# Reordering the first batch of a fused attention-residual and FFN kernel: one root ahead of its gathers, mixing between additions, a square sum ahead of the gates, squared keys at other places

## The chip, the cores and the metric

The kernel runs on one core of one Trainium2 chip. The metric is the device time of one execution in microseconds; lower is better. The kernel before took 779.55 us, the median of three runs (778.33 to 780.54).

## The reference, cut to what matters

The input `x` has 16 batches of 512 rows with 512 columns, `ctx` has 16 batches of 512 rows with 1024 columns. All arithmetic is fp32.

```
x  = x + xattn(layernorm(x), ctx, patch_lens)
x  = x + ffn(layernorm(x))

xattn(e, c, lens):  h  = rmsnorm(e) @ W_in.T + b_in
                    hp = rmsnorm(c)[:, :512]             # mean square over all 1024 columns
                    s  = linear recurrence over rows:  s[t] = a * s[t-1] + gain * hp[t]
                    out[row] = s[plug[row]] + h[row]     # plug from cumulated patch_lens: a gather of rows
ffn(y):             y_prev = y shifted by one row
                    xr = mu_r*y + (1-mu_r)*y_prev ;  xk = mu_k*y + (1-mu_k)*y_prev
                    r  = sigmoid(xr @ W_r.T) ;  k = square(relu(xk @ W_k.T))
                    out = r * (k @ W_v.T)
```

## The kernel before, in words

**Tiling.** A batch is handled as four tiles of 128 rows (T = 4), and its 512 columns as four chunks of 128 (C = 4). Every fp32 product is made of three TensorE matmuls on parts in the type fp32r: high by high, high by low, low by high (`product`, L492 to L496). ScalarE makes the high part with a copy (`copy`, L715); VectorE makes the low part as whole minus high (`low`, L908). One "group" below is such a triple with 512 output columns.

**Stages of batch b.** *Projection* (`project`, L507): x times W_in, 16 groups. *Scan* (`scan`, L516): one group on the first 128 rows of ctx gives the recurrence; VectorE copies it out with the bias (`scan_out`, L914), ScalarE's queue stores it to DRAM (`s_rows`, L757), and GpSimd's queue gathers rows of it and adds them to x in `ring` (`add_patches`, L437, four indirect DMAs, L433). *Addition* (`add_x`, L1028): VectorE adds projection times `rs_a`, the reciprocal root of the first norm, which GpSimd makes (`root_a`, L391). *Second norm*: `stats_b`, `root_b` (L401), `norm_b`; TensorE turns it (`turn`, L589), ScalarE copies it out. *Mixing* (`mixing`, L1014, with ScalarE's `mix_hi`, L767): eight steps, four for xr (0 to 3) and four for xk (4 to 7). Then the *gate product* (xr by W_r, 16 groups), the *key product* (xk by W_k, 16 groups, L558), ScalarE's sigmoid (`gates`, L788) and its relu, square, high part of the keys (`squares`, L798), VectorE's low part of them (`ka_low`, L1064), and the *value product* (L574, 16 groups), whose first two row tiles come ahead of the next scan.

**ctx side.** `squares_c` (ScalarE, L748) squares the 128 x 1024 tile of ctx with a sum; `stats_c` (VectorE, L951), `root_c` (GpSimd, L403) and `scan_input` (VectorE, L957) make the scan's input `u`; `u_high` and `u_low` split it.

**Order.** Each engine executes its own instruction list in the order written out in its `iteration(b)`, with semaphores between engines. Iteration b handles the FFN of batch b, the projection's end and second norm of batch b+1 (`nxt`), and scan and gathers of batch b+2 (`new`). Iterations -1 and 0 are written out with branches of their own (`is_first`); 1 to 12 run in a hardware loop; the last three are written out. The change touches iterations -1 and 0 alone. There, W_r, W_k and W_v are still being split: W_v is staged in the tile `gate`, so `gates(0)` waits until VectorE has made all of `wv_lo` (`weight_lo(WV)`; L795). `squares(b)` of step m = 2 and 3 waits for `ka_low` of step m - 2, whose scratch it writes (L806).

**SyncE's queue**, iteration 0 (L325 to L340): when all four gathers of batch 1 have landed it issues the loads of batch 2: `xt` (1 MB), `ring` (1 MB), `ctx_rows` (0.5 MB), in this order:

```
rows_added(sp, new.plus(-1)) ; ... ; load_xt(new) ; ... ; load_x(new) ; ... ; load_ctx(new)
```

`squares_c(2)` waits for that last load (`reached(act, ctx_loaded, b, 16, 16)`, L749), `stats_c(2)` waits for `squares_c(2)` (L953). The key product's step m waits for `add_x(1, m)` (L566, it writes the bank that `add_x` reads) and at m = 0 chunk by chunk for xk's low parts (L569). The value product at row tile 0 waits for `ka_low(0, m)` before each m (L583).

Of the kernel before, what the change touches and what calls it, by code (L numbers as in the profile page):

```python
# [84 lines left out]
def build(nc, x, x_turned, ctx, patch_lens, w_in, b_in, columns, g_init, w_r, w_k, w_v, out):  # L85

    B, S, D = x.shape
# [11 lines left out]
    with ExitStack() as stack:  # L99
# [133 lines left out]
        def is_first(b, n=0):  # L233
            return b.fixed and b.number() == n
# [117 lines left out]
        def _(pool):  # L352
# [50 lines left out]
            def root_c(b):  # L403
                reached(pool, v_c_done, b, 1, 1)
                reached(pool, u_ready, b.plus(-1), 1, 1)
                nc.gpsimd.tensor_tensor(rs_c[:, :], v_c[:, 1:2], half[:, 0:1], ALU.pow).then_inc(rs_c_done, 1)
# [30 lines left out]
            def add_patches(b):  # L437

                rows_added(pool, b.plus(-1))
                nc.gpsimd.tensor_copy(patch_now[:, :], patch_of[:, bass.ds(b.number(), 1), :].rearrange("p a t -> p (a t)")  # L440
                                      ).then_inc(patch_picked, 1)

                reached(pool, bn_a_done, b, T, T)
                reached(pool, s_stored, b, 16, 16)
                reached(pool, patch_picked, b.plus(-1), 1, 1)
                hold(pool, pool_passed)
                for t in range(T):
                    add_rows(b, t, patch_now[:, t:t + 1])

            def iteration(b):  # L450
                nxt, new = b.plus(1), b.plus(2)
                if nxt.exists(B):
                    root_b(nxt)
                if is_first(b):
                    root_c(new)
                    root_a(new)
                elif new.exists(B) and not is_first(new, 1):
                    root_a(new)
                    root_c(new)
                if new.exists(B):  # L460
                    far(new)
                    add_patches(new)
                if is_first(nxt):
                    root_a(new)

            make_decay(0, P, 0)
            make_blocks()
# [245 lines left out]
        def _(act):  # L713
# [81 lines left out]
                        act.wait_ge(w_lo_ready[WV], C)  # L795
                    nc.scalar.activation(gate[:, t, :], bank[4 + t][:, :], ACT.Sigmoid).then_inc(gate_ready, 1)  # L796

            def squares(b):  # L798

                for m in range(C):  # L800
                    reached(act, k_done, b, C, m + 1)
                    if m == 0:
                        reached(act, mix_lo_ready, b, 2 * C, 2 * C)
                    if m >= 2:

                        reached(act, ka_lo_ready, b, C, m - 1)  # L806
                    nc.scalar.activation(scratch[:, m % 2, :], bank[m][:, :], ACT.Relu).then_inc(relu_ready, 1)  # L807
                    reached(act, relu_ready, b, C, m + 1)
                    nc.scalar.activation(scratch[:, 2 + m % 2, :], scratch[:, m % 2, :], ACT.Square).then_inc(square_ready, 1)  # L809
                    reached(act, square_ready, b, C, m + 1)  # L810
                    copy(ka(b)[0][:, m, :], scratch[:, 2 + m % 2, :]).then_inc(ka_hi_ready, 1)
# [12 lines left out]
            def iteration(b):  # L824
                nxt, new = b.plus(1), b.plus(2)
                if b.exists(B):
                    if is_last(b):
                        mix_hi(b, C, 2 * C)
                        squares(b)
                        gates(b)  # L830
                    elif is_first(b):
                        mix_hi(b, 0, C)
                        weight_hi(WK)
                        mix_hi(b, C, 2 * C)
                        weight_hi(WV)
                        gates(b)
                        squares_c(new)
                    else:
                        mix_hi(b, 0, 2 * C)
                        gates(b)  # L840
                        if new.exists(B):
                            squares_c(new)
                if is_first(b):
                    squares(b)
                    u_high(new)
                if new.exists(B) and not is_first(new, 1):
                    x_hi(new, 0)
                    x_hi(new, 1)
                if b.exists(B) and not is_last(b) and not is_first(b):
                    squares(b)  # L850
                if is_last(nxt):
                    turned_out(nxt)
                    mix_hi(nxt, 0, C)
                if is_first(nxt):
                    x_hi(new, 1)
                    squares_c(new)
                    u_high(new)
                    store_scan(new)
                    turned_out(nxt)
                elif new.exists(B):  # L860
                    if not is_first(b):
                        u_high(new)
                    store_scan(new)
                if nxt.exists(B) and not is_last(nxt) and not is_first(nxt):
                    turned_out(nxt)
# [29 lines left out]
        def _(dve):  # L895
# [173 lines left out]
            def iteration(b):  # L1069
                nxt, new = b.plus(1), b.plus(2)  # L1070
                if is_first(nxt):
                    stats_c(new)
                    for t in range(T):
                        add_x(nxt, t)
                        statistics_b(nxt, t)
                    stats_b(nxt, T)
                    scan_input(new)
                    u_low(new)
                    norm_b(nxt)
                    scan_out(new)  # L1080
                    far(new)
                    dve.sem_inc(far_over, 1)
                    stats_a(new)
                    return
                if b.exists(B):
                    mixing(b, C if is_last(b) else 0, 2 * C if is_last(b) else C + 1)
                if is_first(b):
                    weight_lo(WK)
                if nxt.exists(B):
                    add_x(nxt, 0)  # L1090
                    add_x(nxt, 1)
                if b.exists(B) and not is_last(b):
                    mixing(b, C + 1, 2 * C - 1)
                if nxt.exists(B):
                    add_x(nxt, 2)
                if b.exists(B) and not is_last(b):
                    mixing(b, 2 * C - 1, 2 * C)
                if is_first(b):
                    weight_lo(WV)
                if nxt.exists(B):  # L1100
                    add_x(nxt, 3)
                    stats_b(nxt)
                if is_first(b):

                    ka_low(b, 0)
                    stats_c(new)
                    ka_low(b, 1)
                    scan_input(new)
                    ka_low(b, 2)
                    stats_a(new)  # L1110
                    ka_low(b, 3)
                    u_low(new)
                    norm_b(nxt)
                    gating(b, 0)
                    gating(b, 1)
                    x_lo(new, 0)
                    x_lo(new, 1)
                    scan_out(new)
                    far(new)
                    dve.sem_inc(far_over, 1)  # L1120
                    add_out(b, 0)
                    add_out(b, 1)
                    gating(b, 2)
                    gating(b, 3)
                    add_out(b, 2)
                    add_out(b, 3)
                    return
                if new.exists(B):
                    stats_a(new)
                    stats_c(new)  # L1130
                if nxt.exists(B):
                    norm_b(nxt)
                for m in range(C):
                    if b.exists(B):
                        ka_low(b, m)
                    if new.exists(B):
                        if m in (1, 2):
                            x_lo(new, m - 1)
                        if m == 2:
                            scan_input(new)  # L1140
                if is_last(nxt):
                    mixing(nxt, 0, C)
                if new.exists(B):
                    u_low(new)
                if b.exists(B):
                    gating(b, 0)
                    gating(b, 1)
                if new.exists(B):
                    scan_out(new)
                    far(new)  # L1150
                    dve.sem_inc(far_over, 1)
                if b.exists(B):
                    add_out(b, 0)
                    add_out(b, 1)
                    gating(b, 2)
                    gating(b, 3)
                    add_out(b, 2)
                    add_out(b, 3)
# [131 lines left out]
```

## Time and profile before

| what | us |
|---|---|
| median of three runs | 779.55 |
| the profiled execution, its own time | 780.35 |
| its span (first to last instruction) | 778.8 |
| VectorE busy in the span | 556.2 |
| ScalarE busy | 413.7 |
| GpSimd busy | 175.5 |
| mean granted TensorE clock | 0.992 |

All times in views are from the start of the span, in microseconds. "Busy" of TensorE is modelled: matmuls are pipelined, and each shows about 0.39 us though a new one starts every 0.23 us. A timeline row gives start, duration, engine, source line, operation, tiles, count, and in brackets how long the engine had been idle before it and what released it. Landing times of DMAs are counted from the start of their issue. The granted clock is 1.00 at TensorE's full 2.4 GHz.

### The profile page before, as it was taken

Reading aid. Unit: us, or ns where it says so; the run is one execution under the profiler, and the core shown is the slowest. Engines: PE = TensorE matmul, PEld = TensorE weight load, DVE = VectorE, ACT = ScalarE, POOL = GpSimd, SP = SyncE. Lnnn points to the kernel's source line nnn. Section 1 sums busy time; section 2 is a strip of 40 time slices with the busy share of each in tenths; the row PEclk is TensorE's granted clock in tenths of the full one; section 3 lists DMA queues with packets and bytes.
Section 4 is the critical chain, followed back from the end, with each engine's and each line's share of the span. In section 5 each row is a group of like instructions: output and inputs, shape, how many; then the busy total and the mean of one; then the engine's idle time right before and its main releaser. Section 6 shows DMA issues by size and latency. Waiting matters only on the chain.

```text
span 778.8 us, 10909 instructions
## 1 busy us (share of the span) xinstructions
PE 755.4 (97%) x3462; PEld 621.9 (80%) x3463; DVE 556.2 (71%) x1005; ACT 413.7 (53%) x682; POOL 175.5 (23%) x175
## 2 busy tenths in 40 slices
PE   7878899999999999999999999999999999999997
PEld 4656688888888888888888888888888888888876
DVE  6797886766858677686776769577676967667552
ACT  4346565554546655455664545556454655544760
POOL 6622131313102131220313122131311213130000
PEclk9999999999999999999999999999999999999999
DMA  8556170524417053350705326071531706140011
GB/s 311 147 192 178 41 215 3 153 105 109 149 42 216 0 128 128 88 169 37 213 7 122 135 69 187 14 194 50 121 135 47 209 0 185 72 108 15 1 54 55
DMA packets 42765, 85.73 MB, mean 110 GB/s; under 512 B 3536, under 2 KB 3536, under 8 KB 42704
## 3 DMA queue, kind: packets, MB, share of 16 engines
q1 hardware_dynamic: 30768, 63.74, 21.8%
q0 software_dynamic: 9216, 16.78, 13.6%
q10 hardware_dynamic: 2736, 4.73, 1.8%
q8 instruction: 14, 0.23, 0.1%
q14 instruction: 31, 0.25, 0.1%
HBM read 64.26 MB, written 21.76 MB: 110 GB/s over the span
## 4 chain that ended last, share of the span: by engine, by line
PE 88%; DVE 4%; DMA 2%; issue 2%; ACT 2%; POOL 1%; SPq 0%; DVEq 0%; ACTq 0%; POOLq 0%
PE bank L494 28%; PE bank L495 28%; PE bank L496 28%; PE bank L599 3%; DMA xt<-in_x_turned 1%; POOL ring L433 1%; DMA s_rows<-scanned 1%; DMA ctx_rows<-in_ctx 1%; DVE ring L1034 1%; DVE xk_lo L908 1%; DVE scratch L1004 0%; DVE gate L1062 0%; ACT scratch L809 0%; DVE bn_a L937 0%; ACT scratch L807 0%
## 5 line engine op out<-in xcount | busy, mean ns | idle before, releaser
L433 POOL DMA_INDIRECT ring<-s_rows,patch_now x60 | 101.7, 1695 | 262.7 <-DMA s_rows<-scanned 231.0
L908 DVE TENSOR_TENSOR xr_lo<-scratch,xr_hi 128x512 fp32r<-128x512 f32 x124 | 85.6, 690 | 70.3 <-ACT xr_hi L715 69.8
L1004 DVE SCALAR_TENSOR_TENSOR scratch<-turned,cols,scratch 128x512 f32<-128x512 f32 x128 | 94.5, 749 | 31.5 <-ACT scratch L764 24.9
L715 ACT ACTIVATE turned<-bank 128x512 f32<-128x512 f32 x64 | 33.2, 604 | 137.1 <-PE bank L599 133.5
L494 PE MATMUL bank<-wi_hi,xt_hi 128*128 128x512 f32 x256 | 102.1, 399 | 3.3 <-DVE xt_lo L908 2.7
L494 PE MATMUL bank<-xk_hi,wk_hi 128*128 128x512 f32 x256 | 100.1, 391 | 3.4 <-DVE xk_lo L908 3.4
L494 PE MATMUL bank<-wr_hi,xr_hi 128*128 128x512 f32 x256 | 99.7, 390 | 1.0 <-DVE xr_lo L908 1.0
L495 PE MATMUL bank<-wi_lo,xt_hi 128*128 128x512 f32 x256 | 100.4, 392 | 0.0
L496 PE MATMUL bank<-wi_hi,xt_lo 128*128 128x512 f32 x256 | 100.2, 391 | 0.0
L496 PE MATMUL bank<-xk_hi,wk_lo 128*128 128x512 f32 x256 | 99.6, 389 | 0.0
L495 PE MATMUL bank<-xk_lo,wk_hi 128*128 128x512 f32 x256 | 99.6, 389 | 0.0
L496 PE MATMUL bank<-wr_hi,xr_lo 128*128 128x512 f32 x256 | 99.6, 389 | 0.0
L495 PE MATMUL bank<-wr_lo,xr_hi 128*128 128x512 f32 x256 | 99.6, 389 | 0.0
L494 PE MATMUL bank<-wv_hi,xr_hi 128*128 128x512 f32 x240 | 94.5, 394 | 2.0 <-DVE xr_lo L908 2.0
L495 PE MATMUL bank<-wv_lo,xr_hi 128*128 128x512 f32 x240 | 94.1, 392 | 0.0
L496 PE MATMUL bank<-wv_hi,xr_lo 128*128 128x512 f32 x240 | 94.0, 392 | 0.0
L764 ACT ACTIVATE scratch<-turned,cols 128x512 f32<-128x512 f32 x128 | 89.4, 710 | 0.5
L1062 DVE TENSOR_TENSOR gate<-bank,gate 128x512 f32<-128x512 f32 x64 | 43.9, 691 | 62.3 <-PE bank L496 62.3
L715 ACT ACTIVATE xr_hi<-scratch 128x512 fp32r<-128x512 f32 x124 | 77.9, 628 | 17.6 <-DVE scratch L1004 15.2
L796 ACT ACTIVATE gate<-bank 128x512 f32<-128x512 f32 x64 | 37.7, 595 | 86.0 <-PE bank L496 86.0
L715 ACT ACTIVATE xk_hi<-scratch 128x512 fp32r<-128x512 f32 x64 | 40.4, 632 | 49.3 <-DVE scratch L1004 48.5
L401 POOL TENSOR_TENSOR rs_b<-v_b,half 128x4 f32<-128x4 f32 x16 | 17.0, 1064 | 218.0 <-DVE v_b L1049 218.0
(134 smaller groups left out, 1283.4 us busy)
## 6 DMA issues: line engine op xcount, KB each, us to landing
ring<-in_x SPq DMA_DIRECT2D x16, 1024.0 KB, 7.4
out<-gate SPq DMA_DIRECT2D x64, 256.0 KB, 2.1
xt<-in_x_turned SPq DMA_DIRECT2D x14, 1024.0 KB, 5.2
ctx_rows<-in_ctx SPq DMA_DIRECT2D x16, 512.0 KB, 8.0
s_rows<-scanned ACTq DMA_DIRECT2D x16, 256.0 KB, 2.4
gate<-in_L_xattn_W_in SPq DMA_DIRECT2D x4, 256.0 KB, 6.2
xt<-in_x_turned SPq DMA_DIRECT2D x2, 512.0 KB, 8.0
ring<-in_x_turned SPq DMA_DIRECT2D x1, 1024.0 KB, 12.9
```

Source lines behind the costliest of these rows:

```text
L401: nc.gpsimd.tensor_tensor(rs_b[:, :, 0], v_b[:, :, 0], half[:, :], ALU.pow).then_inc(rs_b_done, 1)
L433: pool.indirect_dma_start(ring[b.slot][:, t, :], None, s_rows[:, :], bass.IndirectOffsetOnAxis(ap=rows, axis=0), compute_op=ALU.add).then_ ...
L494: nc.tensor.matmul(where, lhs_hi, rhs_hi, start=start, stop=False)
L495: nc.tensor.matmul(where, lhs_hi, rhs_lo, start=False, stop=False)
L496: return nc.tensor.matmul(where, lhs_lo, rhs_hi, start=False, stop=stop)
L599: last = nc.tensor.transpose(first_bank(b, t)[:, tile(c)], normed[:, t, c * P:(c + 1) * P], ident[:, :])
L715: return nc.scalar.activation(to, of, ACT.Copy)
L764: nc.scalar.activation(scratch[:, i % 2, :], turned[:, c, 0:S], ACT.Copy, scale=cols[:, 3 + which, c:c + 1]).then_inc(carried, 1)
L796: nc.scalar.activation(gate[:, t, :], bank[4 + t][:, :], ACT.Sigmoid).then_inc(gate_ready, 1)
L908: return nc.vector.tensor_tensor(to, whole, high, ALU.subtract)
L1004: nc.vector.scalar_tensor_tensor(scratch[:, 2 + i % 2, :], turned[:, c, 1:S + 1], cols[:, 1 + which, c:c + 1], scratch[:, i % 2, :], ALU.m ...
L1062: nc.vector.tensor_tensor(gate[:, t, :], bank[4 + t][:, :], gate[:, t, :], ALU.mult).then_inc(gated, 1)
```

## The change

Five moves, all in iterations -1 and 0; nothing is added or removed, only the order within the engines' lists differs.

- GpSimd, iteration -1: `root_a(1)` stands ahead of `add_patches(1)`, that is ahead of the four gathers, and no longer behind them.
- GpSimd, iteration 0: `root_c(2)` stands ahead of `root_b(1)`.
- ScalarE, iteration 0: `squares_c(2)` stands ahead of `gates(0)` (both behind `weight_hi(WV)`); `u_high(2)` stands between `squares` steps 1 and 2 and no longer behind step 3.
- VectorE, iteration 0: `add_x(1,0)`, mixing steps 5 to 7 in one piece, `add_x(1,1)`, `weight_lo(WV)`, `add_x(1,2)`, `add_x(1,3)`.
- VectorE, after that: `stats_c(2)` ahead of `stats_b(1)`, then `scan_input(2)`, `ka_low 0`, `stats_a(2)`, `ka_low 1`, `u_low(2)`, `ka_low 2`, `ka_low 3`.

```diff
@@ gpsimd iteration @@
                 nxt, new = b.plus(1), b.plus(2)
+                if is_first(b):
+                    root_c(new)
                 if nxt.exists(B):
                     root_b(nxt)
                 if is_first(b):
-                    root_c(new)
                     root_a(new)
...
                     far(new)
+                    if is_first(nxt):
+                        root_a(new)
                     add_patches(new)
-                if is_first(nxt):
-                    root_a(new)
@@ scalar @@
-            def squares(b):
+            def squares(b, first=0, last=C):
-                for m in range(C):
+                for m in range(first, last):
...
                         weight_hi(WV)
+                        squares_c(new)
                         gates(b)
-                        squares_c(new)
...
                 if is_first(b):
-                    squares(b)
+                    squares(b, 0, 2)
                     u_high(new)
+                    squares(b, 2, C)
@@ vector iteration, is_first(b) @@
                     weight_lo(WK)
-                if nxt.exists(B):
                     add_x(nxt, 0)
+                    mixing(b, C + 1, 2 * C)
                     add_x(nxt, 1)
-                if b.exists(B) and not is_last(b):
-                    mixing(b, C + 1, 2 * C - 1)
-                if nxt.exists(B):
+                    weight_lo(WV)
                     add_x(nxt, 2)
-                if b.exists(B) and not is_last(b):
-                    mixing(b, 2 * C - 1, 2 * C)
-                if is_first(b):
-                    weight_lo(WV)
-                if nxt.exists(B):
                     add_x(nxt, 3)
+                    stats_c(new)
                     stats_b(nxt)
-                if is_first(b):
+                    scan_input(new)
                     ka_low(b, 0)
-                    stats_c(new)
+                    stats_a(new)
                     ka_low(b, 1)
-                    scan_input(new)
+                    u_low(new)
                     ka_low(b, 2)
-                    stats_a(new)
                     ka_low(b, 3)
-                    u_low(new)
                     norm_b(nxt)
```

The general branch of VectorE's iteration keeps its order; it is only written below the first batch's own list.

## Rows read from the trace of the kernel before

**Rows 1.** The page, part 1: busy time, share of span, instructions.
```profile
PE 755.4 (97%) x3462; PEld 621.9 (80%) x3463; DVE 556.2 (71%) x1005; ACT 413.7 (53%) x682; POOL 175.5 (23%) x175
```
**Rows 2.** Waits of PE from 97 to 779: total, times, longest.
```profile
PE bank L494 <- DVE xk_lo L908: 1.2, 1, 1.2
```
**Rows 3.** Timeline of PE: start, duration, what, idle before.
```profile
65.14 0.39 PE L496 MATMUL bank<-wr_hi,xr_lo 128*128 128x512 f32 x1
66.35 0.47 PE L494 MATMUL bank<-xk_hi,wk_hi 128*128 128x512 f32 x1 [0.82 <-DVE xk_lo L908]
...
70.37 0.48 PE L494 MATMUL bank<-xk_hi,wk_hi 128*128 128x512 f32 x1
...
79.08 0.39 PE L496 MATMUL bank<-xk_hi,wk_lo 128*128 128x512 f32 x1
79.86 0.47 PE L494 MATMUL bank<-wv_hi,xr_hi 128*128 128x512 f32 x1 [0.39 <-DVE xr_lo L908]
...
83.40 0.50 PE L494 MATMUL bank<-wv_hi,xr_hi 128*128 128x512 f32 x1 [0.85 <-DVE xr_lo L908]
...
89.23 0.39 PE L494 MATMUL bank<-u_hi,decay_hi 128*128 128x512 f32 x1
```
**Rows 4.** Stretches: length, busy of the engines, granted clock, DMA share, GB/s.
```profile
80.50:84.00 3.50, 1.87 (x8) 1.00 (x7) 2.71 (x5) 3.37 (x7) 0.00 (x0) 1.00 0.00 0
...
84.50:87.50 3.00, 3.00 (x8) 2.33 (x8) 2.81 (x10) 2.34 (x3) 0.95 (x1) 0.50 0.00 0
```
**Rows 5.** Timeline of DVE, batch 1's first statistics to batch 2's.
```profile
51.76 0.17 DVE L948 TENSOR_SCALAR v_a<-mv_a 128x4 f32<-128x4 f32 x1
...
58.35 2.49 DVE L908 TENSOR_TENSOR wk_lo<-ring,wk_hi 128x512 fp32r<-128x512 f32 x4
63.53 1.41 DVE L1034 SCALAR_TENSOR_TENSOR ring<-bank,rs_a,ring 128x512 f32<-128x512 f32 x2 [2.68 <-POOL rs_a L395]
...
73.28 2.46 DVE L1039 BATCH_NORM_STATS2 bn_b<-ring 128x6 f32<-128x512 f32 x4
...
79.03 0.69 DVE L908 TENSOR_TENSOR xr_lo<-scratch,xr_hi 128x512 fp32r<-128x512 f32 x1 [2.54 <-ACT xr_hi L715]
...
82.65 0.69 DVE L908 TENSOR_TENSOR xr_lo<-scratch,xr_hi 128x512 fp32r<-128x512 f32 x1 [0.46 <-ACT xr_hi L715]
83.26 2.47 DVE L937 BATCH_NORM_STATS2 bn_a<-ring 128x6 f32<-128x512 f32 x4
...
86.38 0.68 DVE L908 TENSOR_TENSOR xr_lo<-scratch,xr_hi 128x512 fp32r<-128x512 f32 x1
```
**Rows 6.** Timeline of POOL: first gather of batch 1, its root.
```profile
54.78 1.79 POOL L433 DMA_INDIRECT ring<-s_rows,patch_now  x1 [8.71 <-DMA s_rows<-scanned]
...
61.76 1.64 POOL L395 TENSOR_TENSOR rs_a<-v_a,half 128x4 f32<-128x4 f32 x1
```
**Rows 7.** DMA issues from 54 to 66: median us to landing.
```profile
ring<-s_rows,patch_now POOLq DMA_INDIRECT x4, 4.8
```
**Rows 8.** Timeline of SP: the loads of batch 2.
```profile
66.26 0.37 SPq L293 DMA_DIRECT2D xt<-in_x_turned  x1
...
67.23 0.50 SPq L296 DMA_DIRECT2D ctx_rows<-in_ctx  x1
```
**Rows 9.** DMA issues from 66 to 76: size, us to landing.
```profile
ctx_rows<-in_ctx SPq DMA_DIRECT2D x1, 512.0 KB, 8.3
```
**Rows 10.** The tile ctx_rows, 0 to 130: its loads' time to landing.
```profile
DMA to landing us min/median/max: 4.6/8.1/8.3
```
**Rows 11.** Timeline of ACT: table load, square sum of ctx, first relu, first high part.
```profile
72.78 1.28 ACT L796 ACT_TABLE_LOAD   x1 [1.13 <-DVE wv_lo L908]
...
76.00 1.08 ACT L751 ACTIVATE ctx_squared<-ctx_rows 128x1024 bf16<-128x1024 f32 x1
...
77.05 0.62 ACT L807 ACTIVATE scratch<-bank 128x512 f32<-128x512 f32 x1
...
78.36 0.63 ACT L715 ACTIVATE xr_hi<-scratch 128x512 fp32r<-128x512 f32 x1
```

More of the change, by code:

```diff
@@ L1127, in iteration @@
                     return
+                if nxt.exists(B):
+                    add_x(nxt, 0)
+                    add_x(nxt, 1)
+                if b.exists(B) and not is_last(b):
+                    mixing(b, C + 1, 2 * C - 1)
+                if nxt.exists(B):
+                    add_x(nxt, 2)
+                if b.exists(B) and not is_last(b):
+                    mixing(b, 2 * C - 1, 2 * C)
+                if nxt.exists(B):
+                    add_x(nxt, 3)
+                    stats_b(nxt)
                 if new.exists(B):
```

## The prediction

> **What bounds the kernel now.** I read the page first: TensorE is busy in 97% of the span [rows 1]. Then the waits of TensorE after the first batches: from 97 us to the end there is one, of 1.2 us [rows 2]. So from there on the product stream is unbroken, and whatever the change does to the time must be done before it: a shift of TensorE's work at about 89 us is carried to the end one for one. The other question is only where batch 0's stream has holes, and TensorE's timeline has them all [rows 3]. The gate product ends at 65.14 + 0.23 = 65.4. The key product starts at 66.35, and its fourth group only at 70.37; from there 38 pitches lead to its last matmul at 79.08, (79.08 - 70.37) / 38 = 0.229 us each, so a group costs 0.69. The value product starts at 79.86 and its third group at 83.40. From there to batch 2's scan at 89.23 stand six groups, 4.1 us at full pitch, and 5.8 were taken. The stretches say why: in 80.5 to 84.0 TensorE is busy for 1.87 of 3.5 us, then the granted clock is 0.50, the lower level of 1.2 GHz, in 84.5 to 87.5 [rows 4]. All holes between 65.4 and 83.4 together: 18.0 us less 18 groups of 0.69 (12.4), thus 5.6, and 1.7 for the clock.
>
> **The change, part by part.**
>
> *The root ahead of the gathers and mixing between additions.* VectorE ends wk_lo at 60.8 and then waits 2.68 us for rs_a, which GpSimd makes behind four gathers [rows 5, 6]. Its input v_a was ready at 51.76 + 0.17 = 51.9 and GpSimd idle [rows 5, 6], so with the root first, at 1.64 us, rs_a is there by about 53.6. The first gather starts at 54.78 and lands 4.8 later, at 59.6 [rows 6, 7]. So add_x(1,0) runs at 60.8, and mixing steps 5 to 7 follow with nothing but themselves: with add_x(1,0) eight instructions of 0.7 us (1.41 for two [rows 5]), to 66.4, with the first xk low at about 62.8, the second 64.2, the third 65.5, the last 66.4. The key product takes its chunks at 65.4, 66.1, 66.8 and 67.4: no hole. It ends at 65.4 + 16 x 0.69 = 76.4 and not at 79.3: 2.9 us sooner. Its later steps need add_x(1,1) at 68.1 (done 67.0), add_x(1,2) at 70.9 (wv_lo goes before it, four instructions like wk_lo's 2.49 [rows 5]: wv_lo done 69.4, the addition 70.1) and add_x(1,3) at 73.6 (done 70.8). The margin at step 2 is 0.8.
>
> The gathers wait for the root, and for the copy of patch_now behind it (4 columns, as the root has, so at most another 1.64): 52.0 to between 53.6 and 55.3, where the first gather started at 54.78 [rows 6]. They move by 0 to 0.5 us. I take nothing, as a plain copy of 4 columns should be well under the root, and keep 0.5 for the range.
>
> *The square sum ahead of the gates.* This is where I expect the loss. squares_c(2) needs the load of ctx_rows. SyncE issues it third of three, after the last gather of batch 1 has landed: xt at 66.26, ctx at 67.23, and it lands 8.3 us after that, at 75.5 [rows 8, 9]. In the kernel before ScalarE is in the gates till 76.00 and finds it there 0.5 us old [rows 11]. Nothing in the change issues it sooner, because the gathers, which the issue follows, start when the scan is stored. Now ScalarE gets to squares_c(2) at about 68, when the last xk high part (65.7) and four copies of wv_hi (0.63 at most each [rows 11]) are out, and stands there for over 7 us. Behind it in its list: the table load and four gates (72.78 to 76.00, 3.22 us, [rows 11]), which could have begun at 69.4 with wv_lo done, and then the squared keys. So:
>
> - squares_c(2) starts at 75.6; it takes 77.05 - 76.00 = 1.05: 76.6.
> - table load and gates 3.22: first relu at 79.9 (before 77.05).
> - relu to high part 78.36 + 0.63 - 77.05 = 1.94 [rows 11]: 81.8. VectorE makes the low part at 81.85, TensorE's first value group follows 0.83 later (79.86 - 79.03 [rows 3, 5]): 82.7 (before 79.86).
>
> *stats_c(2) ahead of stats_b(1).* It makes VectorE wait for the same load, till 76.7. Behind it stand stats_b(1) (four statistics, four small ones and one more, built like stats_a, so 3.12 as worked out below) and scan_input(2) (one instruction like an addition, 0.7): done at 80.5, before the high part of 81.8 is there, so this costs nothing as long as ScalarE is late as well. root_b(1) moves behind it to about 80; norm_b(1), its reader, comes at 89.
>
> *Squared keys' lows.* stats_a(2), 86.38 - 83.26 = 3.12 us [rows 5], now stands between ka_low 0 and ka_low 1, where TensorE waits for each. A low part takes 83.26 - 82.65 = 0.61. ka_low 1 starts at 81.85 + 0.61 + 3.12 = 85.6; u_low and ka_low 2 follow at 86.2 and 86.8. TensorE's third value group follows its low part by 83.40 - 82.65 = 0.75: 87.5, against 83.40. High part 2 is there: relu 1 at 81.7, u_high (a copy of 0.63, as in [rows 11]) from 83.6, relu 2 at 84.1, high part 86.0. Step 3 starts once ka_low 1 is out (86.2), its low part is done at 89.0, and TensorE asks for it at 87.5 + 4 x 0.69 = 90.3. u_low is no longer late for anything.
>
> *Sum.* The third value group comes 87.5 - 83.4 = 4.1 us later, although the key product ended 2.9 earlier: TensorE's holes grow from 5.6 to 9.7 us. For the way from there to the scan I keep the 5.8 us with the low clock in it, as TensorE again stands before it, longer than before. norm_b(1) and scan_out(2) come some 4 us later on VectorE, as TensorE itself does, so nothing new is late for TensorE. So +4.1: span 778.8 to 782.9, the profiled execution's 780.35 to 784.45. That execution lies 0.8 over the median; on the median the forecast is 779.55 + 4.1 = 783.65 us.
>
> *Bounds.* Clock: if no low stretch falls on the six groups, 1.7 us less; if all 18 matmuls are at half speed, 18 x 0.229 = 4.1 over full pitch, 2.4 more than now. Landing of ctx: each us moves the end by one; the loads of this tile took 4.6 to 8.3 [rows 10]. 4.6 would put the landing at 71.8, the end 3.7 sooner. I take 8.3, which is this very load, behind 2 MB in the same queue. Its end can't be much later. Table load: up to 1.28 less if it should run under the wait, which the program order speaks against.
>
> On this the trace shows one load of 1.28 us, after an idle of 1.13, with the gates right behind it [rows 11]. The Trainium skill (ScalarE: Activation LUTs, "What ACT_TABLE_LOAD costs") gives every switch a drain of about 1380 ns beside the 1283 ns of the load. The load agrees; a drain is not seen in the gates' row, but it could have lain in the idle before the load. In the changed kernel the load stands right behind squares_c(2), and such a drain would be in the open: by that page the sum would be 1.4 more, 785.0. I go by the row.
>
> **Rivals.**
>
> *A: the load of ctx is there in time, and the holes close.* It decides at the landing: the third value group comes 12.0 us after it (87.5 - 75.5), so any landing before 71.4 is a gain. With ctx there at 67.7 the gates would end at 69.4 + 3.2 = 72.6, the first high part at 74.5. VectorE would be done with add_x(1,3) at 70.8, stats_b and scan_input at 74.6, ka_low 0 at 75.2; the first value group follows the key product at 76.4; ka_low 1 after stats_a at 78.4, third group at 80.4 (83.4 before): 3.0 less, and 4.7 with the clock held: 774.9 to 776.6. For it: the key product does end 2.9 sooner. Against it: the landing is 4 us off [rows 8, 9], and even the shortest load of this tile misses the point by 0.4.
>
> *B: the wait is there, but most of it is given back.* The low stretch ends within the long hole (-1.7) and the load is a little early (up to -1): +1.4 to +2.3, 781 to 781.9, no measurable change. For it: the hole before the first value group is over 6 us, long enough to hold a stretch of the 3 us seen. Against it: TensorE does only two groups between 82.7 and 87.5, which is less than it did before the drop at 84.
>
> *C: the clock stays low until the scan.* Up to 2.4 more than now, and the gathers up to 0.5 later: +5.3 to +7.0, 784.8 to 786.5. For it: two holes in a row. Against: in the kernel before it was low for 3 us only, with TensorE fully busy in them [rows 4].
>
> **How the numbers follow.** Forecast 0.60, A 0.09, B 0.15, C 0.16. This kernel's measurement tells some 0.3%, 2.3 us, from no change: the bounds are 777.2 and 781.9. Faster 0.09 (A); within 0.13 (most of B); slower 0.78. The range for 8 in 10 leaves out A and the end of C: 780.7 to 786.0. The forecast's own range is 782.5 to 784.8.
>
> **What would show it.** rs_a before the first gather and no hole of TensorE between 65.4 and 76.4 would show the first step right. ScalarE idle for some 8 us before ctx_squared, released by the DMA, and the first relu at about 80 show the second; ctx_rows issued much before 67 or landed before 71.4 would make the forecast wrong. A hole of over 6 us before the first value group and one near 3 us before its second, with stats_a(2) in VectorE's row between, show the third. If the granted clock is 1.00 from 87.5 on, the end comes 1.7 us sooner than forecast.

## The result, and the profile after

The changed kernel takes 784.65 us (median of five runs, 783.69 to 786.57); the kernel before, run beside it, 779.53 (777.85 to 780.54). The ratio is 1.0066, interval 1.0052 to 1.0080: 5.1 us slower, by the interval 4.1 to 6.2. Forecast were 783.7 us and +4.1, with a range from 780.7 to 786.0. The profiled execution took 784.65 with a span of 783.1, against 780.35 and 778.8: +4.3. The median lies inside the range, and inside the forecast's own of 782.5 to 784.8.

TensorE's timeline in batch 0, to be laid beside [rows 3]; columns as there:

```profile
65.53 0.39 PE L495 MATMUL bank<-xk_hi,wk_hi 128*128 128x512 f32 x1
...
76.18 0.39 PE L497 MATMUL bank<-xk_hi,wk_lo 128*128 128x512 f32 x1
82.62 0.77 PE L495 MATMUL bank<-wv_hi,xr_hi 128*128 128x512 f32 x1 [6.05 <-DVE xr_lo L910]
...
86.24 0.80 PE L495 MATMUL bank<-wv_hi,xr_hi 128*128 128x512 f32 x1 [2.00 <-DVE xr_lo L910]
...
87.69 0.63 PE L495 MATMUL bank<-wv_hi,xr_hi 128*128 128x512 f32 x1
...
93.55 0.39 PE L495 MATMUL bank<-u_hi,decay_hi 128*128 128x512 f32 x1
```

The key product has no hole and ends at 76.4, 2.9 us sooner than before. Then TensorE stands for 6 us and once more for 2 (forecast: near 3; the first group ran at half speed and filled 0.7 of it); the third value group comes at 87.69 (before 83.40), the scan at 93.55 (before 89.23). ScalarE, beside [rows 11], shows for whom it stands:

```profile
75.41 1.06 ACT L752 ACTIVATE ctx_squared<-ctx_rows 128x1024 bf16<-128x1024 f32 x1 [7.57 <-DMA ctx_rows<-in_ctx]
76.37 0.19 ACT L752 ACTIVATION_READ_ACCUMULATOR ctx_squared<-ctx_rows 128x1 f32 x1
76.57 1.28 ACT L797 ACT_TABLE_LOAD   x1
77.87 2.06 ACT L797 ACTIVATE gate<-bank 128x512 f32<-128x512 f32 x4
79.79 0.63 ACT L808 ACTIVATE scratch<-bank 128x512 f32<-128x512 f32 x1
```

7.57 us idle, released by the load of ctx, with the table load, the gates and the squared keys in line behind it. The load itself is where it was, beside [rows 8, 9]:

```profile
66.29 0.37 SPq L293 DMA_DIRECT2D xt<-in_x_turned  x1
...
67.26 0.50 SPq L296 DMA_DIRECT2D ctx_rows<-in_ctx  x1
```
```profile
ctx_rows<-in_ctx SPq DMA_DIRECT2D x1, 512.0 KB, 8.1
```

VectorE, beside [rows 5], waits for the same load ahead of stats_b(1), and has stats_a(2) between the first two lows:

```profile
60.91 0.74 DVE L1036 SCALAR_TENSOR_TENSOR ring<-bank,rs_a,ring 128x512 f32<-128x512 f32 x1
...
76.59 0.15 DVE L957 TENSOR_SCALAR v_c<-v_c 128x1 f32<-128x1 f32 x1 [5.72 <-ACT ctx_squared L752]
76.66 2.46 DVE L1041 BATCH_NORM_STATS2 bn_b<-ring 128x6 f32<-128x512 f32 x4
...
81.78 0.69 DVE L910 TENSOR_TENSOR xr_lo<-scratch,xr_hi 128x512 fp32r<-128x512 f32 x1 [1.25 <-ACT xr_hi L716]
82.39 2.47 DVE L939 BATCH_NORM_STATS2 bn_a<-ring 128x6 f32<-128x512 f32 x4
...
85.50 0.68 DVE L910 TENSOR_TENSOR xr_lo<-scratch,xr_hi 128x512 fp32r<-128x512 f32 x1
```

The granted clock, beside [rows 4] (length; busy us of PE, PEld, DVE, ACT, POOL; clock; DMA share; GB/s), is at the lower level of 1.2 GHz for longer than before, but most of it lies on idle time:

```profile
76.50:80.50 4.00, 0.07 (x1) 0.00 (x0) 3.72 (x11) 3.94 (x8) 1.13 (x2) 1.00 0.00 0
80.50:84.00 3.50, 1.38 (x3) 0.84 (x3) 2.25 (x5) 3.40 (x7) 0.91 (x1) 0.59 0.02 5
84.00:88.00 4.00, 2.00 (x5) 1.39 (x5) 3.20 (x10) 3.47 (x7) 1.76 (x2) 0.50 0.01 2
88.00:92.00 4.00, 4.00 (x12) 3.10 (x12) 2.52 (x5) 2.09 (x3) 0.00 (x0) 0.58 0.00 0
```

The same stretch of the kernel before that holds its low clock:

```profile
84.00:88.00 4.00, 4.00 (x12) 3.14 (x11) 3.81 (x11) 2.84 (x4) 1.45 (x2) 0.57 0.00 0
```

With only two levels, a mean of 0.57 over 4.0 us is 3.4 us at the lower one. After the change the rows add up to 2.9 + 4.0 + 3.4 = 10.2 us (about 81.2 to 91.4), of which 3.7 us lie behind the start of the third group.

### The profile page after: what moved, and what is told of

Read it like the earlier page. It is cut to its first block, busy times and chain, and to the rows that moved or that the text cites. A ratio compares the mean times of both kernels' runs of the same rounds, so it can differ in the third digit from the quotient of the medians.

```text
span 783.1 us, 10909 instructions
## 1 busy us (share of the span) xinstructions
PE 756.2 (97%) x3462; PEld 623.7 (80%) x3463; DVE 556.3 (71%) x1005; ACT 413.8 (53%) x682; POOL 176.0 (22%) x175
## 4 chain that ended last, share of the span: by engine, by line
PE 87%; DMA 3%; issue 3%; DVE 3%; ACT 1%; POOL 1%; SPq 0%; DVEq 0%; POOLq 0%; ACTq 0%
PE bank L495 28%; PE bank L496 28%; PE bank L497 28%; PE bank L600 3%; DMA ctx_rows<-in_ctx 2%; DMA xt<-in_x_turned 1%; DMA ring<-s_rows,patch_now 1%; DVE bn_a L939 1%; POOL ring L433 1%; DVE gate L1064 0%; DVE xk_lo L910 0%; DVE scratch L1006 0%; DVE gate L935 0%; ACT turned L716 0%; SPq L299 0%
## 5 line engine op out<-in xcount | busy, mean ns | idle before, releaser
L1006 DVE SCALAR_TENSOR_TENSOR scratch<-turned,cols,scratch 128x512 f32<-128x512 f32 x128 | 94.5, 749 | 34.6 <-ACT scratch L765 17.7
L716 ACT ACTIVATE turned<-bank 128x512 f32<-128x512 f32 x64 | 33.4, 605 | 138.4 <-PE bank L600 138.3
L1064 DVE TENSOR_TENSOR gate<-bank,gate 128x512 f32<-128x512 f32 x64 | 43.9, 690 | 65.2 <-PE bank L497 65.2
```

The lines of the kernel that those rows point to most:

```text
L716: return nc.scalar.activation(to, of, ACT.Copy)
L1006: nc.vector.scalar_tensor_tensor(scratch[:, 2 + i % 2, :], turned[:, c, 1:S + 1], cols[:, 1 + which, c:c + 1], scratch[:, i % 2, :], ALU.m ...
L1064: nc.vector.tensor_tensor(gate[:, t, :], bank[4 + t][:, :], gate[:, t, :], ALU.mult).then_inc(gated, 1)
```

## The experiments

**How the traces are compared.** The start of the program varies from execution to execution: VectorE copies batch 1's scan out (L919 or L921, later lines where a kernel has more) between 46.5 and 49.2 us, in kernels that don't differ ahead of it. From the scan of batch 2 to the end of the span, on the other hand, it is 778.8 - 89.23 = 689.6 us before, 783.1 - 93.55 = 689.6 after, and 689.5 to 689.9 in all ten experiments. So what a kernel did is read from the stretch between the two, counted from the copy's start. "Chain" is from squares_c(2)'s start to the third value group. Two limits: each column of times comes from one execution of each kernel, and the medians do not always follow it. The scan of e9 comes 2.5 us sooner than before and that of e10 2.0 us, while both medians are level. And the experiments ran in three groups (e1 to e4, e5 to e7, e8 to e10), each with its own runs of the kernel before, so medians of different groups are compared through the ratios below.

| kernel | copy at | squares_c(2) at | 1st value group, from copy | 3rd | scan 2 | chain | median us | ratio to before (interval) |
|---|---|---|---|---|---|---|---|---|
| before | 47.77 | 76.00 | 32.1 | 35.6 | 41.5 | 7.4 | 779.5 | |
| changed | 47.61 | 75.41 | 35.0 | 40.1 | 45.9 | 12.3 | 784.65 | 1.0066 (1.0052 to 1.0080) |
| e1 | 48.67 | 76.17 | 33.4 | 38.4 | 43.9 | 10.9 | 783.3 | 1.0050 (1.0036 to 1.0065) |
| e2 | 48.91 | 76.55 | 34.9 | 39.9 | 46.2 | 12.3 | 785.43 | 1.0071 (1.0054 to 1.0087) |
| e3 | 47.88 | 75.04 | 31.0 | 36.1 | 42.3 | 8.9 | 781.33 | 1.0029 (1.0019 to 1.0040) |
| e4 | 47.45 | 75.93 | 32.3 | 35.8 | 42.2 | 7.4 | 780.5 | 1.0014 (1.0002 to 1.0025) |
| e5 | 46.49 | 69.30 | 30.0 | 35.1 | 41.1 | 12.3 | 778.41 | 0.9991 (0.9978 to 1.0004) |
| e6 | 48.52 | 68.43 | 28.5 | 32.7 | 38.3 | 12.8 | 776.93 | 0.9966 (0.9951 to 0.9981) |
| e7 | 47.29 | 76.79 | 28.6 | 30.4 | 34.7 | | 774.17 | 0.9936 (0.9916 to 0.9957) |
| e8 | 48.94 | 81.20 | 31.2 | 33.1 | 37.5 | | 777.83 | 0.9975 (0.9966 to 0.9984) |
| e9 | 49.22 | 76.09 | 30.7 | 34.7 | 39.0 | 7.9 | 779.8 | 1.0008 (0.9994 to 1.0022) |
| e10 | 47.89 | 74.78 | 30.7 | 34.3 | 39.5 | 7.4 | 779.4 | 1.0000 (0.9990 to 1.0011) |

Each experiment ran beside the kernel before, whose medians there were 779.44 to 779.79.

**e1: gates first.** On ScalarE:

```diff
                         weight_hi(WV)
-                        squares_c(new)
                         gates(b)
+                        squares_c(new)
```

> The changed kernel with squares_c(2) put back behind gates(0) on ScalarE; all else as changed. Theory L (ScalarE stands for the landing of ctx at 75.4, and table load and gates, 3.2 us, come behind it): the first relu moves from 79.8 to 76.5. But stats_c(2) still stands ahead of stats_b(1) on VectorE, so the first low part can't start before 80.4; groups of the value product at 81.3, 84.9 and 86.1 (changed: 82.6, 86.2, 87.7). 1.5 us faster than the changed kernel, some 3 us slower than before. Rival V (only VectorE's new order costs): no difference to the changed kernel. Rival S (only ScalarE's order costs): all 4.3 us of span come back.

The chain shrank from 12.3 to 10.9, the third group comes 1.6 us sooner than in the changed kernel (38.4 against 40.1), and the median by 1.35; the intervals of the two ratios overlap, so it is the trace that shows the gain. Theory L had 1.5; against before it is 3.9 slower, where 3 was expected. Rivals V and S are both out: something came back, but not all. The wait for the load is still in front of the squared keys:

```profile
76.17 1.06 ACT L752 ACTIVATE ctx_squared<-ctx_rows 128x1024 bf16<-128x1024 f32 x1 [1.88 <-DMA ctx_rows<-in_ctx]
```

**e2: stats_b(1) first.** On VectorE:

```diff
-                    stats_c(new)
                     stats_b(nxt)
+                    stats_c(new)
```

> The changed kernel with stats_b(1) put back ahead of stats_c(2) on VectorE. Theory L: no difference to the changed kernel (within 0.3 us), since ScalarE gives the first high part at 81.7 and VectorE had 1.25 us to spare there. Rival V: 1 us or more comes back.

The first and third value groups lie as in the changed kernel (34.9 and 39.9 against 35.0 and 40.1). Undone alone, this edit gives nothing; its median is 0.8 higher, within the intervals, and its scan 0.3 later.

**e3: both edits.**

> Both of the two before together: gates ahead of squares_c(2), stats_b(1) ahead of stats_c(2). Left of the change: the front half, stats_a(2) between the first two lows, u_high early. Theory L: first relu 76.5, first low part 78.5, value groups at 79.3, 83.0, 84.2: 3.5 us faster than the changed kernel, 0.8 us slower than before; the 0.8 is stats_a(2) less the 0.5 by which the chain starts sooner. Rival S: as fast as before or faster.

4.0 us less than the changed kernel in the third group, 3.3 less in the median. Against e1 the median is 2.0 lower: e2's edit, worth nothing alone, is worth 2 us once ScalarE is early. Against before it is 0.4 us late in the third group and 0.8 in the scan, as expected; the median is 1.9 higher (by the interval 1.5 to 3.1), where 0.8 was expected, and the other 1.1 is not explained. Rival S is out. The two waits for one load cover each other: undone singly they gave 1.35 us and nothing, together 3.3.

**e9: stats_a(2) behind low 3**, on top of e3:

```diff
                     ka_low(b, 0)
-                    stats_a(new)
                     ka_low(b, 1)
                     u_low(new)
                     ka_low(b, 2)
                     ka_low(b, 3)
+                    stats_a(new)
```

> e3_both with stats_a(2) moved behind low 3, so that it no longer stands between the first two lows; u_high and u_low stay early. My prediction priced it as 3.12 us between the groups. But ScalarE gives the high parts only every 1.83 us, and 0.52 more for u_high: from the first value group to the third 4.2 us, where e3_both has 5.07. So 0.9 us faster than e3_both and level with the kernel before. Rival: the whole 3.1 us come back, 2.3 us faster than before.

From first to third value group 4.0 us, against 5.1 in e3; the median is 1.6 lower by the ratios and level with before, so the rival's 2.3 us are out. So the 3.1 us of statistics cost 1.0 in the chain, the rest lay under ScalarE's pace, one relu every 1.8 us and 2.3 with u_high between:

```profile
77.14 0.58 ACT L808 ACTIVATE scratch<-bank 128x512 f32<-128x512 f32 x1
...
78.95 0.58 ACT L808 ACTIVATE scratch<-bank 128x512 f32<-128x512 f32 x1
...
81.28 0.58 ACT L808 ACTIVATE scratch<-bank 128x512 f32<-128x512 f32 x1
```

**e4: the front half alone** (root, mixing, wv_lo as changed, the rest as before) and **e10: the root alone**, which is the kernel before with

```diff
                     far(new)
+                    if is_first(nxt):
+                        root_a(new)
                     add_patches(new)
-                if is_first(nxt):
-                    root_a(new)
```

> The kernel before with the front half of the change alone: root_a(1) ahead of the gathers, mixing between additions, wv_lo after add_x(1,1). The rest in the old order. The key product ends at 76.4 and not at 79.3. Theory L: only 0.5 us of these 2.9 reach the end, as squares_c(2), which stands ahead of the squared keys in the old order too, must wait for the landing at 75.4, where before it began at 76.0: first relu 76.5, third value group 82.9; 0.5 us faster than before, or 2.2 if the low clock stretch goes. Rival: the 2.9 us arrive in full.

> The kernel before with root_a(1) ahead of the gathers alone. VectorE's wait of 2.7 us goes and the key product ends some 2.4 us sooner (76.9). Theory L: nothing of it reaches the end, as squares_c(2) waits for the landing at 75.4 ahead of the squared keys: within 0.6 us of before. Rival: 2.4 us faster.

In e4 the key product ends at 76.3 and nothing arrives: 1.0014, by the interval 0.2 to 2.0 us slower, where 0.5 faster was expected. The third group is 0.2 us later than before from the copy, the scan 0.7. ScalarE now waits in the old order too:

```profile
75.93 1.06 ACT L751 ACTIVATE ctx_squared<-ctx_rows 128x1024 bf16<-128x1024 f32 x1 [3.03 <-DMA ctx_rows<-in_ctx]
```

The 0.5 us that I had left for it was lost to the gathers, and with them the load, which came 0.8 us later than before, counted from the copy (SyncE's issue at 66.79 - 47.45 = 19.3, before 66.26 - 47.77 = 18.5). In e10 it came 0.8 sooner (65.57 - 47.89 = 17.7), though the edit of the root is the same; so the root's place does not decide it, and it looks like scatter (17.7 to 19.8 over all twelve traces).

In e10 the key product ends at 77.0 (76.9 expected) and the median is that of before, within 0.9 us by the interval: the rival's 2.4 us are out. In its trace, though, the third group comes 1.4 us sooner than before and the scan 2.0, more than the 0.6 allowed for. Of the 1.4, the earlier issue is 0.8, and 0.5 are the time that ctx had lain there unread before. The clock stayed at 1.00, and this execution was also the fastest of twelve.

**e5: the load of ctx first of the three**, the changed kernel otherwise. On SyncE, for batch 2:

```diff
                     rows_added(sp, new.plus(-1))
+                    if is_first(new, 2):
+                        reached(sp, far_over, new.plus(-1), 1, 1)
+                        load_ctx(new)
                     reached(sp, xt_lo_ready, new.plus(-1), 2, 2)
                     load_xt(new)
...
-                    reached(sp, far_over, new.plus(-1), 1, 1)
-                    load_ctx(new)
+                    if not is_first(new, 2):
+                        reached(sp, far_over, new.plus(-1), 1, 1)
+                        load_ctx(new)
```

> The changed kernel, every engine's order kept, with SyncE issuing the load of ctx(2) first of the three and not last, still after the last gather. Theory L: issued at 66.3 and ahead of 2 MB it lands some 4.6 us later, at 70.9, not 75.4; all of the chain comes 4.5 us sooner: first relu 75.3, value groups at 78.1, 81.7, 83.0: 4.5 us faster than the changed kernel, 0.3 faster than before. Rival V (VectorE's order is the cost): no change. Rival: the landing is no earlier because all three share the bandwidth: no change either, and the landing row shows it.

This is the cleanest test of the load: no compute engine's order is touched. The load took 3.2 us and not 8.1, and the two others paid for it with 6.7 and 8.8 us, where the changed kernel has 5.1 and 7.4:

```profile
xt<-in_x_turned SPq DMA_DIRECT2D x1, 1024.0 KB, 6.7
ring<-in_x SPq DMA_DIRECT2D x1, 1024.0 KB, 8.8
ctx_rows<-in_ctx SPq DMA_DIRECT2D x1, 512.0 KB, 3.2
```
```profile
69.30 1.06 ACT L756 ACTIVATE ctx_squared<-ctx_rows 128x1024 bf16<-128x1024 f32 x1 [2.81 <-DMA ctx_rows<-in_ctx]
```

The chain is 12.3 us long in both kernels, to 0.02 us (81.59 - 69.30 and 87.69 - 75.41), and the end moved with the landing: 5.0 us in the third group from the copy, and 5.8 between the medians by the ratios (4.5 expected). Rival V and the rival of shared bandwidth are out. So the changed kernel's end hangs on the landing of this one load. The loss against the kernel before is that more work stands behind that landing: the chain is 12.3 us and not 7.4. With the load 5 us sooner the kernel is still only level with before.

**e6: the load of ctx as soon as the scan of batch 1 is stored**, the changed kernel otherwise. As e5, but ahead of the wait for the gathers:

```diff
+                    if is_first(new, 2):
+                        reached(sp, s_stored, new.plus(-1), 16, 16)
+                        reached(sp, far_over, new.plus(-1), 1, 1)
+                        load_ctx(new)
                     rows_added(sp, new.plus(-1))
```

> The changed kernel with the load of ctx(2) issued when the scan of batch 1 is stored (54.0), ahead of the gathers' landing. Theory L with rival A of the prediction as its consequence: squares_c(2) without a wait at 67.8, gates to 72.6, first high part 74.5, then VectorE sets the pace: value groups at 76.4, 79.1, 80.4, the third 3.0 us before that of the kernel before; with the clock held 4.7. 775 to 776.6 us. It may lose up to 1.3 us, if 0.5 MB among the gathers delays them. Rival V: stays at about 784.

Rival A of the prediction made real: squares_c(2) runs at 68.43 with no wait, and the third group is 3.0 us ahead of before, as worked out there. The median gained is 2.6 and not up to 4.7; at 776.93 it lies just above the 775 to 776.6 expected. The clock was low again in the six groups (5.6 us from the third group to the scan). The gathers were later (xt issued 19.8 us from the copy, before 18.5), but that this load among them is the reason is not shown: in e5, with no load among them, the first issue came at 19.6.

**e7: an order for the landing as it is.** The front half of the change, the old order of GpSimd's roots in iteration 0, and behind it

```diff
 scalar:
                         weight_hi(WV)
+                        squares(b, 0, 1)
                         gates(b)
-                        squares_c(new)
...
-                    squares(b)
+                    squares(b, 1, 3)
+                    squares_c(new)
+                    squares(b, 3, C)
                     u_high(new)
 vector, behind add_x(nxt, 3):
+                    ka_low(b, 0)
+                    stats_b(nxt)
+                    ka_low(b, 1)
+                    statistics_a(new, 0)
+                    ka_low(b, 2)
+                    stats_c(new)
+                    statistics_a(new, 1)
+                    scan_input(new)
+                    ka_low(b, 3)
+                    u_low(new)
+                    stats_a(new, 2)
```

VectorE's list stands in place of the old one, from `stats_b(nxt)` to `u_low(new)`. `statistics_a(new, t)` is one of the four statistics of `stats_a(new)`, and `stats_a(new, 2)` the rest of it.

> An order written for the landing at 75.4: the changed front half; ScalarE: squared keys 0 ahead of the gates, 1 and 2 behind them, then squares_c(2), 3, u_high; VectorE: low 0, stats_b(1), low 1, one statistics of batch 2, low 2, stats_c(2), one more, scan_input(2), low 3, u_low, the rest of stats_a(2). If theory L is the whole of it: value groups 0 to 2 at 76.4, 77.1, 77.9 without a hole, no low clock, scan at about 82: 6.5 to 7.2 us faster than before, 772.5 to 773. Rival: VectorE or ScalarE give it back before the turn of batch 1 (scan_out(2) late at 89): under 5 us.

It beats both kernels: 774.17 us, 5.4 less than the kernel before beside it (by the interval 3.3 to 6.5), and some 10 less than the changed one (10.1 by the ratios). Its profiled execution has a span of 771.9 and reaches the scan 6.7 us sooner from the copy, as expected, and the granted clock is 1.00 from 60 to 96 us. The median gives 5.4 and misses the 772.5 to 773 expected by 1.2; its interval doesn't exclude the rival's "under 5", the trace does. TensorE's waits of batch 0, from 55 to 97 us, are down to one:

```profile
PE bank L494 <- DVE xr_lo L910: 0.2, 1, 0.2
```

**e8: the back half of e7 alone**, on the kernel before's front half.

> The kernel before with the back half of the new order alone (squared keys 0 ahead of the gates, squares_c(2) between steps 2 and 3, stats_b(1) behind low 0, stats_a(2) in pieces); root_a(1) and the mixing as before. Theory L: the key product ends at 79.3 as before, gates end at 76.2, low 1 is out at 78.6 and low 2 at 80.5; value groups at 79.5, 80.1, 80.7, scan at about 85: 4.2 us faster than before with the clock held. The front half, worth nothing alone, is then worth the other 2.5 us of the new order. Rival: the back half alone is worth all of it (7 us), the front half nothing anywhere.

4.0 us sooner at the scan (4.2 expected), but only 2.0 in the median (by the interval 1.2 to 2.7); the other half is not explained. The rival, all 7 us from the back half, is out. So the front half gives nothing on the old back half (e4, e10), but 2.8 us at the scan (37.5 less 34.7), and 3.0 between the medians by the ratios, on one that does not stand for the load.

## Why the prediction was right

- *The front half.* rs_a before the gathers, add_x(1,0) at 60.9, xk lows in time, key product from 65.5 to 76.4 without a hole. All as worked out. That its 2.9 us would be swallowed is shown by e4, also for the old order.
- *squares_c(2) ahead of the gates.* Landing 75.4 (75.5 forecast), first relu 79.79 (79.9), first value group 82.62 (82.7). e5 shows that the end hangs on this landing: it moved, and the value groups moved by the same 5.0 us. e1 and e3 show that it is the order which puts the gates behind it.
- *stats_c(2) ahead of stats_b(1).* Nothing, as long as ScalarE is late: e2. e1 and e3 show the hidden price, 2.0 us in the median and 2.4 in the third group, once it is not.
- *stats_a(2) between the lows.* In the changed kernel low 1 starts at 85.50 (85.6 forecast) and the third group at 87.69 (87.5). The sum is right, but e9 shows that I would have overrated the edit had I named its share as 3.1 us: with it gone, ScalarE's 1.8 us a step and u_high's 0.5 set the pace, and 1.0 comes back.
- *The clock.* I kept the 5.8 us from the third group to the scan, and they are 5.86. That hit is luck in part. I had argued from a low stretch of 3 us; it lasted 10.2 us, began in the hole before the first value group, and 3.7 us of it happened to fall on the six groups, as 3.4 did before. Rival C, a clock low for longer, came true in the length and not in the cost. In the other traces the same stretch takes between 4.2 us (e9) and 6.4 us (e4). Holes alone do not settle it: from 75 to 90 us TensorE waits 2.0 us in the kernel before and the clock falls; in e10, with the same order behind the key product, it waits 3.8 us and the clock stays at 1.00. What sets it is open. The second group, at half speed, delayed the third by 0.2 (its low part was made at 86.71, and 0.75 later is 87.46).
- *The size.* The profiled executions differ by 4.3 us, 0.2 more than the sum, and the 0.2 are those of the third group. The medians differ by 5.1, and 4.1 is at the interval's lower end: the time of the profiled execution was forecast within 0.2 us (784.45), the median missed by 1.0 (783.65). A term that could fill the gap is the clock: the mean granted clock of the five changed runs is 0.981 to 0.991, of the runs of the kernel before beside the experiments it is 0.987 to 0.998. How much of the low clock falls on busy groups in a run without a profile isn't recorded, so this stays open.
- *The drain.* The table load starts 0.01 us behind the read of the accumulator, and the first gate 0.02 us behind the load. The 1.28 us are the whole price in this kernel. The Trainium skill (ScalarE: Activation LUTs, "What ACT_TABLE_LOAD costs") adds a drain of about 1380 ns to each switch, an estimated 1.4 us more here; the rows disagree.

## What to carry to other kernels

An in-order engine should be given an instruction that waits for a load only where the load has landed, counted from the trace, and two waits for the same load on two engines hide each other, so that undoing one shows little or nothing (here 1.35 us and none, both together 3.3). Before moving work to the front, find the last thing released: here time gained in a product (2.9 us) was worth nothing until the order behind it no longer stood for the load. A small load that others need first is worth trying at the head of its queue: here it landed 4.9 us sooner.

## What the runs showed that was not expected

- The order of three loads issued within 1 us on one queue decided which landed first: 0.5 MB took 3.2 us at the head and 8.1 behind 2 MB, while the first 1 MB took 5.1 us at the head and 6.7 behind the 0.5.
- What differs between the twelve traces without an edit that explains it lies ahead of the second scan: in the first 50 us (copy of batch 1's scan at 46.5 to 49.2), from there to SyncE's issue behind the gathers (17.7 to 19.8 us) and in the granted clock of batch 0's end; the 689.5 us behind the second scan repeat to 0.4 us. Each kernel has one trace, so how much a single kernel scatters isn't shown. e10 and e9 had no low stretch on their six groups (from third group to scan 5.2, of which 0.8 is a hole, and 4.2 us), where before took 5.8 with it.
